# A windowed-attention and mixture-of-experts kernel: 1/std spread by TensorE instead of through DRAM, gate rows from transposes, and a new order of work

## What is computed

```
x = x + attention(norm_over_channels(x))     # windows of 8 x 8 pixels, 4 heads of 16, relative bias, softmax, projection
t = pixels as tokens of 64 channels
p = softmax(norm(t) @ router_w + router_b)   # 8 experts; the best two, their p scaled to sum 1
t = t + sum over those two of p * (norm(t) @ expert_w[e] + expert_b[e])
```

## Time and profile before

| | |
|---|---|
| time, median of 3 runs | 1263.94 us (1258.61 to 1264.2) |
| the profiled execution | 1263.9 us, its span 1262.0 us |
| mean granted clock of TensorE | 0.938 of full speed |
| busy: PE | 1095.4 us, 87% of the span |
| busy: DVE | 883.5 us, 70% |
| busy: ACT | 698.2 us, 55% |
| busy: POOL | 438.5 us, 35% |
| moved by transfers | 219.77 MB |

### The profile page before, as it was taken

The page is one execution under the profiler, slowest core; times in us unless marked ns, Lnnn a source line. Parts: engine busy times, 40 slices in busy tenths (PEclk is TensorE's granted clock), DMA queues, the critical chain, the costliest instruction groups (busy, mean ns, idle before and its releaser), DMA issues.

```text
span 1262.0 us, 38803 instructions
## 1 busy us (share of the span) xinstructions
PE 1095.4 (87%) x16678; PEld 570.0 (45%) x16678; DVE 883.5 (70%) x1398; ACT 698.2 (55%) x1153; POOL 438.5 (35%) x359
## 2 busy tenths in 40 slices
PE   4787989998989998999999998999899898998754
PEld 3444444444545444444444444544444454444311
DVE  3345787777778777776677777787778876677552
ACT  1376556656666565656655666665566655654410
POOL 1002333234344333243433324433433334433443
PEclk7599899999999899999988999999999999999877
DMA  5115678888777678787767878777778887765777
GB/s 166 35 41 121 157 181 197 198 197 187 186 191 192 170 190 204 182 210 163 181 170 178 205 192 201 176 193 170 183 181 208 201 193 170 176 161 136 173 181 171
DMA packets 71017, 219.77 MB, mean 174 GB/s; under 512 B 13632, under 2 KB 26560, under 8 KB 54336
## 3 DMA queue, kind: packets, MB, share of 16 engines
q1 hardware_dynamic: 70848, 217.30, 71.9%
HBM read 177.15 MB, written 23.33 MB: 159 GB/s over the span
## 4 chain that ended last, share of the span: by engine, by line
DMA 39%; PE 30%; issue 12%; SPq 6%; POOL 6%; DVE 3%; ACT 3%; POOLq 0%; ACTq 0%
DMA xs<-in_x 18%; DMA gz<-gates_dram 17%; PE bank L588 6%; PE bank L471 5%; PE bank L504 4%; SPq L343 3%; PE bank L459 3%; SPq L323 3%; DMA gates_dram<-gsb 3%; POOL gz L896 3%; PE bank L486 2%; PE bank L521 2%; PE bank L528 2%; DVE ob L1017 2%; PE bank L538 2%
## 5 line engine op out<-in xcount | busy, mean ns | idle before, releaser
L896 POOL TENSOR_TENSOR gz<-gz,tt 128x1024 f32<-128x1024 f32 x96 | 242.8, 2529 | 327.6 <-DMA gz<-gates_dram 327.6
L588 PE MATMUL bank<-gz,wex 64*64 64x512 f32 x2048 | 294.4, 652 | 19.2 <-DVE gz L1009 9.9
L1009 DVE TENSOR_TENSOR gz<-gz,tt 128x1024 f32<-128x1024 f32 x160 | 224.2, 1403 | 110.2 <-DMA gz<-gates_dram 110.1
L987 DVE TENSOR_REDUCE mx<-bank 128x16 f32<-128x1024 f32 x128 | 156.2, 1220 | 81.3 <-PE bank L471 81.3
L471 PE MATMUL bank<-km,qs 32*64 32x128 f32 x4096 | 178.3, 287 | 7.4 <-issue 7.1
L504 PE MATMUL bank<-cst,probs 128*128 128x128 f32 x1024 | 171.9, 292 | 9.5 <-ACT pt L738 3.9
L504 PEld LDWEIGHTS bank<-cst,probs 128*128 128x128 f32 x1024 | 113.2, 144 | 134.1 <-issue 108.1
L738 ACT ACTIVATE pt<-bank 128x512 f32<-128x512 f32 x256 | 151.4, 591 | 24.5 <-PE bank L504 22.2
L471 PEld LDWEIGHTS bank<-km,qs 32*64 32x64 f32 x4096 | 113.3, 135 | 105.9 <-issue 89.0
L869 POOL TENSOR_TENSOR tt<-prj,xs 128x512 f32<-128x512 f32 x64 | 80.8, 1285 | 225.5 <-ACT prj L755 225.5
L994 DVE TENSOR_TENSOR probs<-bank,mx 128x1024 f32<-128x1024 f32 x128 | 156.0, 1219 | 2.2
(11 more groups left out here) (97 smaller groups left out, 1357.5 us busy)
## 6 DMA issues: line engine op xcount, KB each, us to landing
gz<-gates_dram SPq DMA_DIRECT2D x256, 512.0 KB, 12.0
xs<-in_x SPq DMA_DIRECT2D x32, 512.0 KB, 14.3
rstd<-std_dram SPq DMA_DIRECT2D x64, 256.0 KB, 4.0
tx<-tt SPq DMA_DIRECT2D x128, 128.0 KB, 3.9
out<-ob SPq DMA_DIRECT2D x128, 128.0 KB, 13.1
gates_dram<-gsb SPq DMA_DIRECT2D x32, 192.0 KB, 2.1
grow<-gates_dram SPq DMA_DIRECT2D x192, 32.0 KB
gz<-in_rel SPq DMA_DIRECT2D x1, 2048.0 KB, 9.4
```

Source lines behind the costliest of these rows:

```text
L588: last = mm(bank[64 * x:64 * x + 64, Y_BANK + a, :], wex[64 * a:64 * a + 64, e, :], gz[64 * a:64 * a + 64, s.pair(e)[1], e % 2, x * CH:(x ...
L896: tt_(gz[:, k, e % 2, :], gz[:, k, e % 2, :], tt[s.buf(4)][:, :], op=ALU.mult).then_inc(z_pool, 1)
L987: red(mx[g % 2][:, :], two_banks(S_BANK).rearrange("p (c k) -> p c k", k=N), axis=AX_X, op=ALU.max).then_inc(max_done, 1)
L1009: tt_(gz[:, k, e % 2, :], gz[:, k, e % 2, :], tt[s.buf(4)][:, :], op=ALU.mult).then_inc(z_dve, 1)
```

## The change

1. The first norm's 1/std no longer goes through DRAM. ACT makes a rounded copy in every second row with a sign (`signed_std`), DVE adds the exact value there (`split_std`), so that high part and rest stand in rows of their own, and PE spreads them into PSUM banks 0 and 1 with a selection matrix in four products of 256 columns (`spread_std`). `scale_x` reads the factor from there. `channel_sums` and `variance` move from `s[0]` to `s[1]`; the selection matrix is made at the start from two shifted copies (`norm_setup`, with one transfer inside SBUF). `write_std` and `spread_std` of SP go.
2. The gates are placed so that four transposes give all four forms in rows of their own: rows 0 to 95 are the plain gates for the bias, kept in SBUF (`gt`), rows 96 to 127 the gates times 1/std, which alone go to DRAM. `load_gate_rows` goes. The bias matrix `eb` is loaded in twelve small pieces into another layout.
3. All eight experts of a strip are summed in one step, that of `s[6]`, a step after their products; the store comes in `s[7]`, so there are 39 steps. The router moves to the end of step `s[3]`, `values` 0 and 1, transposes 2 and `scores_left` 3 of a strip to the end of step `s[2]`. POOL makes both residuals in step `s[3]`.

The core of the diff:

```diff
-    LAST_STAGE = 6
+    LAST_STAGE = 7
...
-            0: [("lgT", 4, L_ready, 2), ("K", 2, k_ready, 2), ("Q", 2, q_ready, 1), ("stats", 0, var_done, 1),
-                ("gT", 4, gsb_ready, 1), ("proj", 3, prj_ready, 1), ("V", 2, v_ready, 2)],
-            1: [("router", 4, lg_ready, 1), ("K", 2, k_ready, 2), ("Q", 2, q_ready, 1), ("proj", 3, prj_ready, 1),
-                ("V", 2, v_ready, 2)],
+            0: [("lgT", 4, L_ready, 2), ("K", 2, k_ready, 2), ("Q", 2, q_ready, 1), ("stats", 1, var_done, 1),
+                ("gT", 4, gsb_ready, 2), ("V", 2, v_ready, 2), ("proj", 3, prj_ready, 1), ("spread", 1, xr_ready, 1)],
+            1: [("K", 2, k_ready, 2), ("Q", 2, q_ready, 1), ("V", 2, v_ready, 2), ("proj", 3, prj_ready, 1),
+                ("spread", 1, xr_ready, 1), ("router", 3, lg_ready, 1)],
...
+                sp.wait_ge(gsb_ready, s.count(2, 1))
+                sp.dma_start(gates_dram[s.buf(4)].rearrange("m (x t) -> x m t", x=2), gt_rs[s.buf(2)][96:P, :]
+                             ).then_inc(gates_written, 16)
...
             def late_loads():
                 sp.dma_start(rel_int, rel.rearrange("k q -> (k q)").partition_broadcast(P)).then_inc(rel_loaded, 16)
-                for dst, src in ((wproj[:, :], proj), (rbias[:, :], router_bias), (ebraw, expert_bias)):
+                for dst, src in ((wproj[:, :], proj), (rbias[:, :], router_bias)):
                     sp.dma_start(dst, src).then_inc(late_loaded, 16)
+                sp.wait_ge(sel_set, 1)
+                for row in range(0, 3 * 32, E):
+                    a, x = row // E % 2, row // (2 * E) % 2
+                    sp.dma_start(ebraw[row:row + E, a, C * x:C * x + C], expert_bias[E * a:E * a + E, C * a:C * a + C]
+                                 ).then_inc(late_loaded, 16)
+                sp.wait_ge(sel_made, 1)
+                sp.dma_start(sel_low[2:P, :], sel_high[0:P - 2, :]).then_inc(sel_moved, 16)
...
+            def spread_std(st, s):
+                pe.wait_ge(low_ready, s.count(1, 1))
+                if s.c == 0:
+                    pe.wait_ge(sel_ready, 1)
+                free(st, "spread", 0)
+                free(st, "spread", 1)
+                for c in range(4):
+                    last = mm(two_banks(PRE)[:, c * QT:(c + 1) * QT], sel[:, c, :], rstd_hl[:, :], start=True, stop=True,
+                              skip_group_check=True)
...
             def transpose_gates(st, s):
-                pe.wait_ge(gp_ready, s.count(2, 2))
+                pe.wait_ge(gp_ready, s.count(4, 4))
                 free(st, "gT", 0)
-                nc.tensor.transpose(bank[:, PRE, 0:P], gp_rs[:, :], cv("ident"))
-                for part in range(2):
-                    last = nc.tensor.transpose(bank[:, PRE, P + P * part:2 * P + P * part],
-                                               gp_hl[:, part, :].bitcast(F32), cv("ident"))
+                for ttl in range(4):
+                    last = nc.tensor.transpose(bank[:, PRE, 128 * ttl:128 * ttl + 128],
+                                               gp[:, ttl, :, :, :].rearrange("p k x m -> p (k x m)").bitcast(F32),
...
             def expert_bias_rows(s):
-                pe.wait_ge(grow_loaded, s.count(96, 96))
+                pe.wait_ge(gsb_ready, s.count(2, 2))
                 for a in range(2):
-                    last = mm(bank[:, Y_BANK + a, :], eb[:, :], grow[s.buf(2)][:, a, :], start=False, stop=True,
+                    last = mm(bank[:, Y_BANK + a, :], eb[0:96, a, :], gt[s.buf(2)][0:96, :], start=False, stop=False,
                               skip_group_check=True)
-                last.then_inc(y_full, 1)
...
+            def signed_std(s):
+                if s.c == 0:
+                    act.wait_ge(sel_ready, 1)
+                act.wait_ge(rstd_done, s.count(1, 1))
+                wait(act, low_ready, s.count(1, 0))
...
             def move_gates(s):
                 act.wait_ge(gt_full, s.count(1, 1))
-                wait(act, gates_written, s.count(16, 0))
-                af(gsb[:, :, :].rearrange("p s t -> p (s t)"), bank[:, PRE, 0:3 * P], ACT.Copy).then_inc(gsb_ready, 1)
+                wait(act, gates_written, s.count(16, 16, lag=2))
+                af(gt_rs[s.buf(2)][96:P, :], bank[96:P, PRE, :], ACT.Copy).then_inc(gsb_ready, 1)
+                wait(act, eb_done, s.count(1, 1, lag=2))
+                af(gt[s.buf(2)][0:96, :], bank[0:96, PRE, :], ACT.Copy).then_inc(gsb_ready, 1)
...
                 wide = lambda ap: ap.unsqueeze(2).broadcast_to([P, 16, E])
-                v = lambda t: t[:, :, :].rearrange("p (x a) e -> p x a e", a=2)
-                spot = lambda ap: ap.rearrange("p (a e x) -> p x a e", a=2, e=E)
+                tiles = lambda t: t[:, :, :].rearrange("p (x t a) e -> p t x (a e)", x=2, a=2)
+                part = lambda k: gp[:, :, k, :, :]
                 pool.wait_ge(g_ready, s.count(2, 2))
                 tt_(ga[:, :, :], oh1[:, :, :], wide(g1[:, :]), op=ALU.mult).then_inc(gate, 1)
                 tt_(gb[:, :, :], oh2[:, :, :], wide(g2[:, :]), op=ALU.mult).then_inc(gate, 1)
                 pool.wait_ge(gate, s.count(GATE, 2))
                 wait(pool, gt_full, s.count(1, 0))
+                tt_(part(0), tiles(ga), tiles(gb), op=ALU.add).then_inc(gate, 1)
                 tt_(gsum[:, :, :], ga[:, :, :], gb[:, :, :], op=ALU.add).then_inc(gate, 1)
-                tt_(spot(gp_hl[:, 0, :]), v(ga), v(gb), op=ALU.add).then_inc(gate, 1)
+                tt_(part(2), tiles(ga), tiles(gb), op=ALU.add).then_inc(gp_ready, 1)
+                pool.wait_ge(gate, s.count(GATE, 4))
+                tt_(part(1), tiles(gsum), part(0).bitcast(F32), op=ALU.subtract).then_inc(gp_ready, 1)
                 pool.wait_ge(rs_ready, s.count(1, 1))
-                pool.wait_ge(gate, s.count(GATE, 4))
-                tt_(spot(gp_rs[:, :]), v(gsum),
-                    rs[:, :].rearrange("p (x a) -> p x a", a=2).unsqueeze(3).broadcast_to([P, 8, 2, E]),
-                    op=ALU.mult).then_inc(gp_ready, 1)
-                tt_(spot(gp_hl[:, 1, :]), v(gsum), spot(gp_hl[:, 0, :].bitcast(F32)),
-                    op=ALU.subtract).then_inc(gp_ready, 1)
+                pool.wait_ge(gp_ready, s.count(4, 2))
+                tt_(gsum[:, :, :], gsum[:, :, :], wide(rs[:, :]), op=ALU.mult).then_inc(gp_ready, 1)
...
+            def norm_setup():
+                dve.wait_ge(sel_made, 1)
+                dve.wait_ge(sel_moved, 16)
+                tt_(sel[:, :, :].rearrange("p c m -> p (c m)"), sel_high[:, 0:4 * P], sel_low[:, 0:4 * P], op=ALU.add)
+                copy(is_low[:, :], sel_low[:, 4 * P:4 * P + 1])
+                nc.vector.tensor_scalar(low_sign[:, :], sel_low[:, 4 * P:4 * P + 1], -2.0, 1.0, ALU.mult,
+                                        ALU.add).then_inc(sel_ready, 1)
...
+            def split_std(s):
+                dve.wait_ge(signed_ready, s.count(1, 1))
+                wait(dve, spread_full, s.count(1, 0))
+                nc.vector.scalar_tensor_tensor(out=rstd_hl[:, :], in0=var[:, :], scalar=is_low[:, 0:1],
+                                               in1=signed[:, :].bitcast(F32), op0=ALU.mult, op1=ALU.add
+                                               ).then_inc(low_ready, 1)
...
-                dve.wait_ge(rstd_loaded, s.count(32, 32))
+                dve.wait_ge(spread_full, s.count(1, 1))
...
-                    windows(rstd), op=ALU.mult).then_inc(xr_ready, 1)
+                    windows(two_banks(PRE)), op=ALU.mult).then_inc(xr_ready, 1)
...
             def finish(s):
-                dve.wait_ge(y_full, s.count(1, 1))
+                dve.wait_ge(e_done, s.count(E, E))
+                dve.wait_ge(eb_done, s.count(1, 1))
...
```

More of the change, by code:

```diff
@@ L909, in _ @@
                 if s[5].on:
+                    gated(s[5], 4)
                     gated(s[5], 7)
@@ L1113, in _ @@
                     pick_one(s[4])
+                if s[3].on:
+                    shift(s[3], 3)
+                if s[4].on:
                     top_two(s[4])
                     pick_two(s[4])
+                if s[3].on:
+                    normalise(s[3], 0)
+                if s[4].on:
+                    gates(s[4])
                 if s[2].on:
@@ L1132, in _ @@
                     shift(s[2], 1)
[L1133 to L1134 removed]
+                if s[5].on:
+                    gated(s[5], 3)
                 if s[3].on:
                     normalise(s[3], 3)
+                if s[2].on:
+                    row_max(s[2], 2)
+                if s[1].on:
+                    split_std(s[1])
+                if s[5].on:
+                    gated(s[5], 5)
+                if s[2].on:
+                    shift(s[2], 2)
+                if s[1].on:
+                    scale_x(s[1])
+                if s[6].on:
+                    finish(s[6])
                 if s[5].on:
                     gated(s[5], 6)
[L1139 to L1142 removed]
                 if st.c == 0:
+                    norm_setup()
                     late_setup()
```

334 lines of the change are left out of this document (161 added, 173 removed).

## The result

The changed kernel takes 1272.58 us (median of 20 runs, 1260.64 to 1284.53) against 1263.51 for the kernel before (20 runs): a ratio of 1.0057, 95% interval 1.0032 to 1.0083. It is half a per cent slower, where 1218 and "faster" had been forecast. A ratio in this document leaves out the runs that lie more than some 1.5% above the fastest of their kernel, while a median is over all of them, so that the two can differ where runs are few. Two profiles of the changed kernel are used: the first has a span of 1277.8 us, a second one (run e1_same, the same text) 1269.5; that of before has 1262.0. Their spread is not small, so a cause has to show in more than one.

The account below looks back on a forecast made before the run. TensorE was taken as the bound, 92% busy in the middle. From 1263.9 us, 29 steps at 34.3 instead of 36.1 gave -52, the start +11, the end -5: 1218 us, range 1185 to 1262.

Parts of the forecast that it names:

- With no long hole left, 0.2 for the clock: 34.3 instead of 36.1: Middle steps: 34.1 us plus 0.2 for the clock gives 34.3 instead of 36.1, times 29: -52 us.
- clock below 0.97 in the middle: Sign that the forecast is wrong: TensorE's granted clock in the middle of the run falls under 0.97.
- The sum for a step, 34.1: Full step at full clock: TensorE's work of 32.9 us plus remaining waits of 1.2 us makes 34.1.
- The spread: Four new 256-column fp32r products on TensorE: 0.64 to 1.28 us a step, 0.8 taken.
- `keys` and `channel_sums`: TensorE's holes ahead of these lines: 0.1 us instead of 1.52, and 0 instead of 1.27.
- `queries`: Step start: GpSimd's product 1 meets VectorE's token statistics, 1.4 us late, ACT holds `move_k`, and `queries` waits 0.8 us.
- held at full length: Rival: products 1 and 7 block VectorE for their whole length; 36.0 us a step, 1267 us, no change; chance 0.13.
- Transfers: Ten of some 32 a strip go, about 0.8 of 6.8 MB; a gz pair alone takes 7.3 us, 4.9 each behind it.
- late-gates rival: Rival: gz pair 3 lands late, product 7 delays residuals, square and router; 38.2 us a step, 1331 us; chance 0.10.
- The start: Before the first `keys`: onehots 7.7 us later, strip 0's norm +3.3; +11 us, between +6 and +14, nothing hides it.
- The end: Step 34 shortens by 5 us, last experts follow their products as now (0): -5 us, between -10 and +3.
- F: Experiments' theory: TensorE's next instruction block queues behind data, TensorE runs dry at the block's end, the clock falls behind the stop.

Follow-up runs that it names:

- e4: Changed kernel with GpSimd's product 1 made behind `place_gates`, not as the step begins: 1244.72 us, 0.9755 of the kernel before.
- e13_shift: Changed kernel with 32 extra small TensorE products once ahead of the onehots, moving later instructions half a block on: 1261.14 us, 0.9933 of the kernel before.
- e10_paced: Changed kernel with stores, x load and pair 1 issued later, spreading the same bytes over the step: 1234.81 us, 0.9639 of the kernel before.
- e12_paced_start: Changed kernel with the transfers paced as in e10_paced, and `late_setup` ahead of `norm_setup` on VectorE: 1236.85 us, 0.9776 of the kernel before.
- e2_light: Changed kernel without seven eighths of the x load (from strip 4) and token swap (from strip 2): 1241.66 us, 0.9821 of the kernel before.
- e5: Changed kernel with one more 512 KB transfer a strip, to spare DRAM, ahead of the token swap: 1272.31 us, 1.0054 of the kernel before.
- e8: Changed kernel with product 1 behind `place_gates`, `late_setup` ahead of `norm_setup`, and the token swap held to mid-step: 1238.13 us, 0.9803 of the kernel before.

## Why the prediction was wrong

- **The step that failed** is "With no long hole left, 0.2 for the clock: 34.3 instead of 36.1". It took every hole of the profile for a wait of the program, and held the clock's loss to be theirs. 14 of 29 steps are disturbed by stops that no wait makes and take 38.1; (38.11 - 34.60) x 14 = 49 us, nearly the whole gain forecast. The kernel before had such stops too, 12 of them with 21 us in all, and the forecast left no place for them. Its sign "clock below 0.97 in the middle" came (0.96), and so did "steps of over 35.2" (36.30). None of its rivals had this mechanism.
- **The sum for a step, 34.1**: near for a quiet step, 34.60 and 34.29, and 34.12 in the window above, but partly by luck. TensorE's work in the quiet steps is 32.2 in both profiles (forecast 32.9; before 32.0), and it stands 2.4 and 2.1 us in them (forecast 1.2; before 2.85). Two misses of opposite sign nearly cancel. So of the 1.8 us forecast the quiet steps got 0.3 to 0.6. The holes ahead of `keys` and `channel_sums`, 56 us in the 29 steps of before, lay with 33 of them in disturbed steps.
- **The spread**: 0.8 forecast, from 0.64 to 1.28. Four products pass in 0.56, below the lower bound:

```profile
597.67 0.72 PE L432 MATMUL bank<-rstd_hl,sel 128*128 128x256 f32 x4
598.23 0.63 PE L495 MATMUL bank<-bias_hl,tile_id 128*128 128x512 f32 x2
```

- **`keys` and `channel_sums`**: right, both holes are gone, and with them the eight falls of the clock behind them. **`queries`**: right in mechanism (GpSimd's product 1 holds the statistics, they hold `move_k`), 33.1/24 = 1.4 us a time instead of 0.8. The rows below are VectorE's lines of the changed kernel; in the kernel before the first took 175 ns and the third 578. The rival "held at full length" thus came near in time (1267) and not in mechanism: with its hold gone in e4, the quiet steps gained 0.1.

```profile
L1101 DVE TENSOR_TENSOR mq<-st_ 128x16 f32<-128x16 f32 x32 | 40.3, 1260 | 1.1
L1102 DVE TENSOR_TENSOR vr<-st_,mq 128x16 f32<-128x16 f32 x32 | 13.9, 435 | 1.1
...
L1015 DVE TENSOR_SCALAR var<-var 128x256 f32<-128x256 f32 x32 | 61.5, 1921 | 0.1
```

- **Transfers**: right in size. Moved bytes fell from 219.8 to 192.5 MB, a pair lands in 6.7 us (7 to 8 forecast), so the late-gates rival never began. What was not asked is who else queues there: pair 3, x, the gates and the token swap are now issued within 7 us, and blocks of TensorE's instructions are fetched through the same engines.
- **The start**: +6.4, not +11, inside its bounds of +6 to +14. The first `keys` came where forecast, near 44; what failed is "nothing hides it". The onehots end their wait at 28.29 and `keys` begins near 43.6 (33.28 before), 10.3 later; strips 0 to 2 give 4 back.

```profile
28.29 7.00 PE L391 MATMUL bank<-tb,gz 128*64 128x12 bf16 x256 [17.51 <-DVE gz L984]
...
40.95 1.22 PE L432 MATMUL bank<-rstd_hl,sel 128*128 128x256 f32 x4 [3.80 <-DVE rstd_hl L1021]
43.58 1.98 PE L441 MATMUL bank<-xr,wcen 64*64 64x512 f32 x8 [1.41 <-DVE xr L1031]
```

- **The end**: +4.3, not -5, outside its bounds of -10 to +3. "The last experts follow their products as now: 0" is wrong: they come a step later, TensorE waits 9.20 for the last gates and 8.16 for `finish`, with the work of other strips gone from beside them.

```profile
1236.75 1.11 PE L574 MATMUL bank<-cst,gp 128*128 128x128 f32 x4 [9.20 <-POOL gp L910]
...
1261.48 3.69 PE L597 MATMUL bank<-gz,wex 64*64 64x512 f32 x16 [8.16 <-DVE ob L1068]
```

Shown by experiment: the stops, and the falls of the clock behind them, follow the instruction blocks (e13_shift), and the same bytes spread over the step take 2.2 to 3.6% off with the long waits of the lines unchanged (e10_paced, e12_paced_start). Argued only: that a late block is late because of the data ahead of it. The records of single stops and e2_light speak for it; the extra transfer of e5 and the single one held back in e8 did nothing, and pacing removed fewer stops than F had. Not told apart: how the 49 us divide between stop and clock. Open: why e5's extra transfer did nothing, why e4's order has fewer stops, and why the quiet steps of e10 are shorter. That the changed kernel is slower than the one before at all, by 0.57%, is less than the placing of the blocks moves it.

## What to carry to other kernels

A stop "by issue" inside a run of instructions that has no wait is not the program's: look whether it wanders by a fixed number of instructions from one repetition to the next, and what was issued to the DMA queues just before. Before a gain is forecast from holes, compare quiet repetitions with disturbed ones; what the quiet ones lack is what the holes can be counted on to give back; the rest hangs on what disturbs the others. In a kernel with long code on TensorE, try transfers that are issued spread over the step, each on a semaphore near its use, and not as one burst when slots come free; here that alone took some 2% off.

## What the hardware showed unexpectedly

- TensorE's instructions came in blocks of 16,384 bytes (134 of them) through the DMA engines that carry the data. At the 24 stops of the profile of after, the fetch began 3.1 to 10 us after the block ahead was entered (median over all 105 crossings: 3.07) and took 1.0 to 1.4 us; TensorE stopped for 0.3 to 3.5 us and went on 1.3 to 1.6 us after the landing. The Trainium skill (Runtime: NRT & Kernel Launch, Instruction fetch mechanics) has the blocks of 16 KiB and the queue, and calls the cost of crossing a boundary mostly hidden; here 24 of 105 crossings cost 44 us.
- An operation on 16 elements a partition with two SBUF inputs took 1.26 us in the mean for 0.175 beside GpSimd's product, and a `tensor_scalar` with one input on 256 elements 1.92 for 0.58: with one SBUF input too, VectorE was held.
- A 256-column fp32r product with a new 128x128 weight took 0.14 us in the pass of four; one of 512 columns takes 0.32.
